# Two multiplies of an FP4 quantization moved from VectorE to GpSimd, with alternating buffers

## The chip, the cores and the metric

One Trainium2 chip, all 8 of its cores. Each core runs the same program on one of 8 batch elements of 2048 tokens with 1024 features; nothing is exchanged between cores. The metric is the device time of the slowest core in microseconds. Engines are named as in the profile: PE is TensorE (matmuls), PEld its weight loads, DVE is VectorE, ACT is ScalarE, POOL is GpSimd, SP is SyncE, which only issues DMAs here.

## What is computed

Two layers, each a product of a mixer and a gated feed-forward, added to its input. The change lies in the feed-forward of the first layer, which quantizes all its operands to FP4 in blocks of 16:

```python
xn = layernorm(x)
s  = attention(xn)                                  # stage 1
def fp4_quant_dequant(x):                           # blocks of 16 along the last dim
    scale = max(max|xb| / 6, 1e-12)
    q = GRID[searchsorted(MID, |xb / scale|)] * sign * scale    # grid 0 .5 1 1.5 2 3 4 6
def fp4_linear(x, w):
    return quant(x) @ quant(w).T
h = silu(fp4_linear(xn, w_gate)) * fp4_linear(xn, w_up)         # stage 2, 2816 hidden columns
x = x + s * silu(fp4_linear(h, w_down))
...                                                 # layer 1: a scan (stage 3) and a mixture
                                                    # of 8 experts (stage 4)
```

## The kernel before

The whole program is written once as a "narrative" (`make_l0_attn`, `make_l0_ffn`, `make_l1_attn`, `make_l1_ffn`), which is run once for each engine and emits only that engine's instructions. So each engine executes its instructions in the order in which they stand in the text, and waits only on semaphores: `ved` counts VectorE's steps, `sed` ScalarE's, `ted` TensorE's, `sx`, `sw` the loads. Between stages every engine waits for every semaphore (`phase_barrier`, L107). Stage 2 is `make_l0_ffn` (L582), and it has four loops.

**x tiles** (L631 to L666), 16 tiles of 128 tokens. SP loads the tile into `xt[i % 2]` (L635). `_emit_layernorm` (L554) takes the statistics on VectorE (L555, L556, L558, L560), the root on ScalarE (L564), the reciprocal and a product on VectorE (L567, L569), and normalizes on ScalarE into `q0` (L574). `_emit_quant` quantizes `q0` into `qbf` (bf16, 128x1024). TensorE makes eight 128x128 transposes into a PSUM bank (L656), and ScalarE evacuates it into `xqT` (L661). Before the layer norm of tile i VectorE waits for the transposes of tile i-1 (L641).

**gate/up slices** (L674 to L800), 5 slices of 512 hidden columns and one of 256. For each, 256 rows of the weights at a time are quantized by `_emit_quant2` (L504, two chains interleaved, all of it on VectorE), transposed (L708) and evacuated (L716, L720). Then come 16 token tiles: eight matmuls for gate (L738) and eight for up (L743), Silu on ScalarE (L752), the product on VectorE into one half of `hh` (L756). After every odd tile (a pair is done) VectorE quantizes the pair, `hh` into `hb`: at once as 1024 columns (L766), or in the last slice as two quantizations of 256 columns (L769, L772). TensorE transposes `hb` (L783), and ScalarE evacuates it into `hqT` (L790, L795). In TensorE's order these transposes stand between the matmuls of this pair and those of the next.

**wd rows** (L807 to L847), 8 rows of 128x2816, each loaded by SP into `wdr` (L815, in the space of `q3`, `q4` and what follows) once the last quantization of the row before has ended, and quantized in pieces of 1024, 1024 and 768 columns (L824), with transposes (L835) and an evacuation (L840). Before each piece VectorE waits for the transposes of the one before (L823), since `hb` is written again.

**down** (L851 to L904): matmuls, Silu, gate and residual. The change doesn't touch it.

`_emit_quant` (L468) is a chain of 13 VectorE operations, each reading what the one before wrote. Its last two, L499 and L501, multiply `t2` by the block scales (an operand repeated 16 times) and then `t1` by `t2` into the bf16 output. Everything up to L496 is called the head below, L499 and L501 the tail.

Of the kernel before, what the change touches and what calls it, by code (L numbers as in the profile page):

```python
# [82 lines left out]
def alloc_sems(nc, names):  # L83
# [4 lines left out]
             "ted", "ved", "sed", "std0", "std1", "stx0", "stx1"]  # L88
# [379 lines left out]
def _emit_quant(p, out_bf, t0, t1, t2, blk, W):  # L468
    nb = W // 16
    bm, hs = blk[:, 0:nb], blk[:, nb:2 * nb]  # L470
# [3 lines left out]
    t2 = t2[:][:, 0:W]  # L474
    p.ve.tensor_reduce(bm.rearrange("p (nb one) -> p nb one", one=1), r3(t0),
# [106 lines left out]
def make_l0_ffn(nc, dram, pq, pfx="b_"):  # L582
# [38 lines left out]
    def narrative(p):  # L621
# [6 lines left out]
        ve_q = []  # L628
        te_tr = []
        ve_evac = []  # L630
        for i in range(NT):  # L631
            sl = i % 2
            if i >= 2:
                p.sy.wait_ge(p.ved.h, ve_q[i - 2])
# [8 lines left out]
            se_xn = p.sed.bump()  # L643
            p.ve.wait_ge(p.sed.h, se_xn)
# [28 lines left out]
        se_htr_evac = None  # L673
        for (hs0, hw) in SLICES:  # L674
            nrc = hw // 128
            for gu in range(2):
                for rp in range(nrc // 2):
# [51 lines left out]
            for tc in range(NT):  # L729
# [33 lines left out]
                if se_htr_evac is not None:  # L763
                    p.ve.wait_ge(p.ted.h, te_htr)
                if hw == 512:
                    _emit_quant(p, hb[:, 0:1024], hh[:][:, 0:1024],  # L766
                                q1, q2, blk, 1024).then_inc(p.ved.h, 1)
                else:
                    _emit_quant(p, hb[:, 0:hw], hh[:][:, 0:hw],  # L769
                                q1, q2, blk, hw)  # L770
                    p.ve.drain()
                    _emit_quant(p, hb[:, 512:512 + hw], hh[:][:, 512:512 + hw],  # L772
                                q3, q4, blk, hw).then_inc(p.ved.h, 1)
                ve_hq = p.ved.bump()
# [3 lines left out]
                p.te.wait_ge(p.ved.h, ve_hq)  # L778
# [9 lines left out]
                te_htr = p.ted.bump()  # L788
                p.se.wait_ge(p.ted.h, te_htr)
# [14 lines left out]
        se_wdtr_evac = {}  # L804
        te_wdtr = None
        pi_k = 0
        for rc in range(ND):  # L807
            if rc == 0:
# [10 lines left out]
            if rc == 0:  # L819
                p.ve.wait_ge(p.ted.h, te_htr)  # L820
# [847 lines left out]
```

## Time and profile before

| | us |
|---|---|
| two runs | 6973.5 and 7301.9, median 7137.7 |
| profiled execution | 6957.9 |
| its span on the slowest core (core 0) | 6956.4 |
| spans of the other seven | 6899.7 to 6953.7 |

The profile is that of core 0. It gives for each engine the busy time, for groups of instructions the mean duration, and for idle time of an engine what ended it. Times within the program are counted from the start of the span. Stage 2 runs from about 1486 to 3820 us. A busy TensorE isn't TensorE at its peak: its clock has two levels, 1.2 and 2.4 GHz, and "PEclk" is the share of the higher one that was granted (0.5 is 1.2 GHz).

### The profile page before, as it was taken

Reading aid. Unit: us, or ns where it says so; the run is one execution under the profiler, and the core shown is the slowest. Engines: PE = TensorE matmul, PEld = TensorE weight load, DVE = VectorE, ACT = ScalarE, POOL = GpSimd, SP = SyncE. Lnnn points to the kernel's source line nnn. Section 1 sums busy time; section 2 is a strip of 40 time slices with the busy share of each in tenths; the row PEclk is TensorE's granted clock in tenths of the full one; section 3 lists DMA queues with packets and bytes.
Section 4 is the critical chain, followed back from the end, with each engine's and each line's share of the span. In section 5 each row is a group of like instructions: output and inputs, shape, how many; then the busy total and the mean of one; then the engine's idle time right before and its main releaser. Section 6 shows DMA issues by size and latency. Waiting matters only on the chain.

```text
span 6956.4 us, 45524 instructions; the slowest of 8 cores (6899.7 to 6956.4 us)
## 1 busy us (share of the span) xinstructions
PE 3609.6 (52%) x15560; PEld 1519.5 (22%) x15560; DVE 2292.4 (33%) x3549; ACT 1256.5 (18%) x2020; POOL 54.1 (1%) x67
## 2 busy tenths in 40 slices
PE   2944445420233233242008055626898898898891
PEld 1410101000111111112004022213343343343340
DVE  2121101047665655646672311223121121121122
ACT  1233333321100001010001321112121121111111
POOL 0000000000000000000000000000000000000000
PEclk9855555555566566576559588857999999999996
DMA  4000000001000000000014412160202202202203
GB/s 88 1 12 0 12 0 12 0 31 36 24 12 12 24 0 24 19 6 7 33 39 146 108 22 24 49 179 16 49 1 49 49 1 49 49 1 49 49 1 142
DMA packets 104753, 248.10 MB, mean 36 GB/s; under 512 B 39984, under 2 KB 40496, under 8 KB 103504
## 3 DMA queue, kind: packets, MB, share of 16 engines
q0 software_dynamic: 62720, 84.73, 8.1%
q1 hardware_dynamic: 41808, 160.45, 6.6%
q8 instruction: 131, 2.15, 0.1%
q14 instruction: 94, 0.77, 0.0%
HBM read 287.80 MB, written 41.94 MB: 47 GB/s over the span
## 4 chain that ended last, share of the span: by engine, by line
PE 49%; DVE 19%; ACT 10%; issue 9%; DMA 9%; DVEq 3%; another core or an unknown queue 0%; SPq 0%; POOL 0%; ACTq 0%; POOLq 0%
PE pq L1416 13%; PE pq L1442 13%; PE pq L1085 4%; PE pq L738 3%; DMA d_b2r<-b_row 3%; PE pq L384 3%; ACT a_expA L357 3%; PE pq L743 2%; ACT a_expB L358 2%; PE pq L342 2%; PE pq L386 2%; PE pq L268 2%; DVE b_q L483 1%; DVE b_q L499 1%; DVE b_q L493 1%
## 5 line engine op out<-in xcount | busy, mean ns | idle before, releaser
L1416 PE MATMUL pq<-d_tT,d_w1e 128*128 128x512 bf16 x4096 | 908.6, 385 | 36.2 <-ACT d_hTh L1424 36.2
L1442 PE MATMUL pq<-d_w2e,d_hTh 128*128 128x512 bf16 x4096 | 889.2, 379 | 33.6 <-ACT d_hTh L1424 33.6
L1458 DVE SCALAR_TENSOR_TENSOR d_acc<-pq,d_comb,d_acc 128x512 f32<-128x512 f32 x256 | 192.2, 751 | 1634.8 <-PE pq L1442 1634.8
L1424 ACT ACTIVATE d_hTh<-pq,d_b1s 128x512 bf16<-128x512 f32 x512 | 352.6, 689 | 1236.5 <-PE pq L1416 1236.5
L1416 PEld LDWEIGHTS pq<-d_tT,d_w1e 128*128 128x128 bf16 x4096 | 404.9, 99 | 538.7 <-issue 68.4
L1442 PEld LDWEIGHTS pq<-d_w2e,d_hTh 128*128 128x128 bf16 x4096 | 398.4, 98 | 524.4 <-issue 48.5
L384 PE MATMUL pq<-a_expA,a_vsb 128*65 128x512 bf16 x320 | 194.3, 607 | 571.6 <-DVE a_expB L369 292.5
L366 DVE TENSOR_TENSOR a_expA<-a_expA,a_masks_s 128x512 bf16<-128x512 bf16 x128 | 54.4, 425 | 965.2 <-ACT a_expB L358 965.2
L783 PE MATMUL pq<-b_ident_s,b_hb 128*128 128x128 bf16 x352 | 45.1, 305 | 611.4 <-DVE b_hb L501 611.4
L1085 PE MATMUL pq<-c_xn2T,c_wsl 128*128 128x512 bf16 x1024 | 263.6, 404 | 162.6 <-ACT c_ga L1095 81.0
L357 ACT ACTIVATE a_expA<-pq 128x512 bf16<-128x512 f32 x320 | 191.2, 597 | 665.3 <-PE pq L346 665.3
L708 PE MATMUL pq<-b_ident_s,b_qbf 128*128 128x128 bf16 x352 | 41.0, 310 | 463.6 <-DVE b_qbf L541 463.6
L738 PE MATMUL pq<-b_wgTs,b_xqT 128*128 128x512 bf16 (+1 forms) x768 | 237.2, 469 | 13.9 <-ACT b_wuTs L720 13.9
L756 DVE TENSOR_TENSOR b_hh<-b_sg,pq 128x512 f32<-128x512 f32 (+1 forms) x96 | 61.7, 643 | 476.9 <-ACT b_sg L752 476.9
L386 PE MATMUL pq<-a_expB,a_vsb 128*65 128x512 bf16 x320 | 202.2, 632 | 0.0
L384 PEld LDWEIGHTS pq<-a_expA,a_vsb 128*65 128x65 bf16 x320 | 42.0, 131 | 724.1 <-issue 724.1
L1461 DVE SCALAR_TENSOR_TENSOR d_acc<-d_b2b,d_comb,d_acc 128x512 f32<-128x512 f32 x256 | 192.3, 751 | 19.7 <-issue 0.9
L342 PE MATMUL pq<-a_qT,a_kT 64*128 64x512 bf16 x320 | 192.9, 603 | 4.1 <-DVE a_s0c L445 3.1
L346 PE MATMUL pq<-a_qT,a_kT 64*128 64x512 bf16 x320 | 193.5, 605 | 0.0
L743 PE MATMUL pq<-b_wuTs,b_xqT 128*128 128x512 bf16 (+1 forms) x768 | 190.4, 397 | 0.0
L358 ACT ACTIVATE a_expB<-pq 128x512 bf16<-128x512 f32 x320 | 189.9, 593 | 0.0
L835 PE MATMUL pq<-b_ident_s,b_hb 128*128 128x128 bf16 x176 | 22.6, 306 | 305.2 <-DVE b_hb L501 305.2
(211 smaller groups left out, 3831.4 us busy)
## 6 DMA issues: line engine op xcount, KB each, us to landing
d_w1e<-w1T POOLq DMA_DIRECT2D x8, 4096.0 KB, 28.3
d_w2e<-w2T POOLq DMA_DIRECT2D x8, 4096.0 KB, 29.0
b_wrow<-wgu SPq DMA_DIRECT2D x44, 512.0 KB, 4.1
b_xt<-x SPq DMA_DIRECT2D x32, 512.0 KB, 4.6
b_wdr<-wd SPq DMA_DIRECT2D x8, 1408.0 KB, 6.4
a_xt<-x SPq DMA_DIRECT2D x16, 512.0 KB, 3.4
s<-a_s0c SPq DMA_DIRECT2D x16, 512.0 KB, 2.6
b_st_<-s SPq DMA_DIRECT2D x16, 512.0 KB, 5.5
```

The lines of the kernel that those rows point to most:

```text
L342: p.te.matmul(sa_[:], kT[0:64, hp * S + kc * 128: hp * S + kc * 128 + 128], qT[0:64, hp * S + qt * 512: hp * S + (qt + 1) * 512], start=Tr ...
L346: p.te.matmul(sb_[:], kT[64:128, hp * S + kc * 128: hp * S + kc * 128 + 128], qT[64:128, hp * S + qt * 512: hp * S + (qt + 1) * 512], star ...
L357: p.se.activation(expA[:, esl * 512:(esl + 1) * 512], sa_[:], AF.Exp)
L358: p.se.activation(expB[:, esl * 512:(esl + 1) * 512], sb_[:], AF.Exp) \
L384: p.te.matmul(pq[4][0:65, :], vA, expA[:, esl * 512:(esl + 1) * 512], start=(kc == 0), stop=(kc == nkc - 1))
L386: p.te.matmul(pq[5][0:65, :], vB, expB[:, esl * 512:(esl + 1) * 512], start=(kc == 0), stop=(kc == nkc - 1)) \
L738: p.te.matmul(gb[:, 0:hw], xqT[:, j * S + tc * 128: j * S + (tc + 1) * 128], wgTs[:, j * 512: j * 512 + hw], start=(j == 0), stop=(j == ND ...
L743: inst = p.te.matmul(ub[:, 0:hw], xqT[:, j * S + tc * 128: j * S + (tc + 1) * 128], wuTs[:, j * 512: j * 512 + hw], start=(j == 0), stop=( ...
L1085: inst = p.te.matmul(bank[:], wsl[sl][:, (w * ND + j) * 128:(w * ND + j + 1) * 128], xn2T[:, j * S + ch * 512: j * S + (ch + 1) * 512], st ...
L1416: inst = p.te.matmul(bank[:], w1e[:, j * MOE_H + hc * 128: j * MOE_H + (hc + 1) * 128], tT[:, j * S + hf * 512: j * S + (hf + 1) * 512], s ...
L1424: p.se.activation(hTh[:, hc * 512:(hc + 1) * 512], bank[:], AF.Gelu, bias=b1s[:, e * 16 + hc: e * 16 + hc + 1]) \
L1442: inst = p.te.matmul(bank[:], hTh[:, j * 512 + tr * 128: j * 512 + (tr + 1) * 128], w2e[:, j * D + dh * 512: j * D + (dh + 1) * 512], star ...
```

## The change

`_emit_quant` keeps its head on VectorE, and its two last multiplies are issued on GpSimd. A new semaphore, `pod`, counts GpSimd's steps: GpSimd waits for the head, multiplies, waits for its own first multiply, multiplies again. `_emit_quant` gets an offset into `blk` (the block scales) and two optional waits: `wait_pod`, which VectorE waits for before the head, and `gp_wait_ted`, which GpSimd waits for before it writes. TensorE now waits for `pod` ahead of the transposes.

In the x tiles `qbf`'s two halves, `blk`'s two parts and the pairs `q1,q2` and `q3,q4` alternate; VectorE doesn't wait for the transposes any more; SP reloads `xt` when ScalarE has normalized it. For the pairs of token tiles the same two sets of buffers alternate (`hb` is still one). `_emit_quant2` stays as it is, but waits for all of GpSimd's work. For `wd` only `q1,q2` are used, so that each head waits for the tail before it; the next `wd` row is loaded once the last head of a row has ended.

```diff
 def _emit_quant(...):
+    if wait_pod:
+        p.ve.wait_ge(p.pod.h, wait_pod)
     ...
     p.ve.tensor_scalar(t2.bitcast(I32), t2.bitcast(I32), 0x7F800000, None,
-                       ALU.bitwise_xor)
-    p.ve.drain()
-    p.ve.tensor_tensor(r3(t2), r3(t2), b3(hs[:]), ALU.mult)
-    p.ve.drain()
-    return p.ve.tensor_tensor(out_bf, t1, t2, ALU.mult)
+                       ALU.bitwise_xor).then_inc(p.ved.h, 1)
+    ved_head = p.ved.bump()
+    p.gp.wait_ge(p.ved.h, ved_head)
+    if gp_wait_ted:
+        p.gp.wait_ge(p.ted.h, gp_wait_ted)
+    p.gp.tensor_tensor(r3(t2), r3(t2), b3(hs[:]), ALU.mult) \
+        .then_inc(p.pod.h, 1)
+    p.gp.wait_ge(p.pod.h, p.pod.bump())
+    p.gp.tensor_tensor(out_bf, t1, t2, ALU.mult).then_inc(p.pod.h, 1)
+    pod_tail = p.pod.bump()
+    return ved_head, pod_tail
...
 # x tiles
             if i >= 2:
-                p.sy.wait_ge(p.ved.h, ve_q[i - 2])
+                p.sy.wait_ge(p.sed.h, se_xn_prev[i - 2])
...
-            if i >= 1:
-                p.ve.wait_ge(p.ted.h, te_tr[i - 1])
...
-            _emit_quant(p, qbf[:, 0:D], q0[:], q1, q2, blk, D).then_inc(p.ved.h, 1)
-            ve_q.append(p.ved.bump())
+            t12 = (q1, q2) if i % 2 == 0 else (q3, q4)
+            vh, pt = _emit_quant(
+                p, qbf[:, (i % 2) * D:(i % 2) * D + D], q0[:], t12[0], t12[1],
+                blk, D, boff=(i % 2) * 256,
+                wait_pod=(quv[i - 2][1] if i >= 2 else None),
+                gp_wait_ted=(te_tr[i - 2] if i >= 2 else None))
...
-            p.te.wait_ge(p.ved.h, ve_q[i])
+            p.te.wait_ge(p.pod.h, pt)
...
 # weights of a slice
-                        blk, [0, 256], D)
+                        blk, [0, 256], D,
+                        wait_pod=(p.pod.v if p.pod.v else None))
...
 # pairs of token tiles
-                if se_htr_evac is not None:
-                    p.ve.wait_ge(p.ted.h, te_htr)
+                par = hq_k % 2
+                t12 = (q1, q2) if par == 0 else (q3, q4)
+                wp = hq_pt.get(hq_k - 2)
+                gwt = hq_te.get(hq_k - 1)
                 if hw == 512:
-                    _emit_quant(p, hb[:, 0:1024], hh[:][:, 0:1024],
-                                q1, q2, blk, 1024).then_inc(p.ved.h, 1)
+                    vh, pt = _emit_quant(p, hb[:, 0:1024], hh[:][:, 0:1024],
+                                         t12[0], t12[1], blk, 1024,
+                                         boff=par * 256, wait_pod=wp,
+                                         gp_wait_ted=gwt)
...
-                p.te.wait_ge(p.ved.h, ve_hq)
+                p.te.wait_ge(p.pod.h, pt)
...
 # wd
-                if te_wdtr is not None:
-                    p.ve.wait_ge(p.ted.h, te_wdtr)
-                _emit_quant(p, hb[:, 0:cw], wdr[:][:, c0:c0 + cw], q1, q2, blk, cw) \
-                    .then_inc(p.ved.h, 1)
-                ve_wdq = p.ved.bump()
+                vh, pt = _emit_quant(
+                    p, hb[:, 0:cw], wdr[:][:, c0:c0 + cw], q1, q2,
+                    blk, cw, boff=0,
+                    wait_pod=wd_pt.get(pi_k - 1),
+                    gp_wait_ted=(te_wdtr if pi_k >= 1 else te_htr))
+                wd_pt[pi_k] = pt
+                ve_wdq = vh
...
-                p.te.wait_ge(p.ved.h, ve_wdq)
+                p.te.wait_ge(p.pod.h, pt)
```

## Rows read from the trace of the kernel before

**Rows 1.** The page, busy us of each engine (share of the span), x instructions

```profile
PE 3609.6 (52%) x15560; PEld 1519.5 (22%) x15560; DVE 2292.4 (33%) x3549; ACT 1256.5 (18%) x2020; POOL 54.1 (1%) x67
```

**Rows 2.** Windows view: stretch, length, busy us of each engine, PEclk, DMA share, GB/s

```profile
1486.00:1757.00 271.00, 15.76 (x126) 12.22 (x127) 197.00 (x304) 39.83 (x48) 0.47 (x1) 0.50 0.10 35
1757.00:3326.00 1569.00, 480.12 (x2244) 244.47 (x2242) 953.71 (x1396) 147.13 (x236) 0.00 (x0) 0.63 0.04 14
3326.00:3656.00 330.00, 23.64 (x181) 17.27 (x180) 231.33 (x312) 23.57 (x26) 0.00 (x0) 0.50 0.10 38
```

**Rows 3.** Waits, 1486 to 3660 us: engine, tile, line, releaser: total us, times, longest

```profile
PE pq L783 <- DVE b_hb L501: 611.4, 48, 13.4
...
PE pq L835 <- DVE b_hb L501: 305.2, 24, 18.5
...
PE pq L656 <- DVE b_qbf L501: 262.8, 16, 29.5
```

**Rows 4.** Timeline, an x tile: start us, us, engine, line, op, operands, count [idle]

```profile
1603.65 0.69 DVE L496 TENSOR_SCALAR b_q<-b_q 128x1024 int32<-128x1024 int32 x1
...
1605.71 1.23 DVE L501 TENSOR_TENSOR b_qbf<-b_q 128x1024 bf16<-128x1024 f32 x1
1607.16 0.77 PEld L656 LDWEIGHTS pq<-b_ident_s,b_qbf 128*128 128x128 bf16 x8 [16.09 <-issue]
1607.19 1.01 PE L656 MATMUL pq<-b_ident_s,b_qbf 128*128 128x128 bf16 x8 [15.86 <-DVE b_qbf L501]
1608.30 1.03 ACT L661 ACTIVATE b_xqT<-pq 128x1024 bf16<-128x1024 bf16 x1 [12.93 <-PE pq L656]
1608.31 0.69 DVE L555 BATCH_NORM_STATS2 b_blk<-b_xt 128x6 f32<-128x512 f32 x1 [1.37 <-PE pq L656]
...
1610.20 0.20 ACT L564 ACTIVATE b_blk<-b_blk 128x1 f32<-128x1 f32 x1 [0.88 <-DVE b_blk L560]
```

**Rows 5.** Timeline, two pairs of 1024 columns

```profile
1876.43 3.29 PE L738 MATMUL pq<-b_wgTs,b_xqT 128*128 128x512 bf16 x8
...
1879.55 1.89 PE L743 MATMUL pq<-b_wuTs,b_xqT 128*128 128x512 bf16 x8
...
1894.35 0.68 DVE L496 TENSOR_SCALAR b_q<-b_q 128x1024 int32<-128x1024 int32 x1
...
1897.86 0.77 PEld L783 LDWEIGHTS pq<-b_ident_s,b_hb 128*128 128x128 bf16 x8 [13.46 <-issue]
...
1898.70 3.62 PE L738 MATMUL pq<-b_wgTs,b_xqT 128*128 128x512 bf16 x8
...
1902.11 2.40 PE L743 MATMUL pq<-b_wuTs,b_xqT 128*128 128x512 bf16 x8
```

**Rows 6.** Timeline, a pair of the 256-column slice

```profile
3264.41 0.42 DVE L475 TENSOR_REDUCE b_blk<-b_hh 128x16 f32<-128x256 f32 x1 [0.16 <-issue]
...
3267.88 0.28 DVE L496 TENSOR_SCALAR b_q<-b_q 128x256 int32<-128x256 int32 x1
...
3274.25 0.34 PEld L783 LDWEIGHTS pq<-b_ident_s,b_hb 128*128 128x128 bf16 x4 [11.28 <-issue]
```

**Rows 7.** Timeline, end of one `wd` row and start of the next

```profile
3446.18 0.55 DVE L496 TENSOR_SCALAR b_q<-b_q 128x768 int32<-128x768 int32 x1
...
3448.90 0.33 SPq L815 DMA_DIRECT2D b_wdr<-wd  x1
...
3455.32 1.22 DVE L475 TENSOR_REDUCE b_blk<-b_wdr 128x64 f32<-128x1024 f32 x1 [6.52 <-DMA b_wdr<-wd]
...
3463.48 0.69 DVE L496 TENSOR_SCALAR b_q<-b_q 128x1024 int32<-128x1024 int32 x1
...
3468.14 1.22 DVE L475 TENSOR_REDUCE b_blk<-b_wdr 128x64 f32<-128x1024 f32 x1 [1.37 <-PE pq L835]
```

**Rows 8.** Groups by line, 1900 to 4700 us: wider and narrower multiplies and additions

```profile
L1113 DVE TENSOR_TENSOR c_gb_<-c_gd,c_gb_ 128x2048 f32<-128x2048 f32 x8 | 18.3, 2293 | 361.6 <-ACT c_gd L1105 361.6
...
L1157 DVE TENSOR_TENSOR c_s1t<-pq,c_obb 128x512 f32<-128x512 f32 x16 | 11.1, 691 | 81.5 <-DMA c_xt<-xn 74.7 <-PE pq L1136 6.8
```

More of the change, by code:

```diff
@@ L465, in make_l0_attn, with _emit_quant @@
     return narrative
-def _emit_quant(p, out_bf, t0, t1, t2, blk, W):
+def _emit_quant(p, out_bf, t0, t1, t2, blk, W, boff=0, wait_pod=None,
+                gp_wait_ted=None):
     nb = W // 16
-    bm, hs = blk[:, 0:nb], blk[:, nb:2 * nb]
+    bm, hs = blk[:, boff:boff + nb], blk[:, boff + nb:boff + 2 * nb]
     r3 = lambda ap: ap.rearrange("p (nb w) -> p nb w", w=16)
@@ L496, in _emit_quant, with _emit_quant2 @@
     p.ve.tensor_scalar(t2.bitcast(I32), t2.bitcast(I32), 0x7F800000, None,
-                       ALU.bitwise_xor)
-    p.ve.drain()
-    p.ve.tensor_tensor(r3(t2), r3(t2), b3(hs[:]), ALU.mult)
-    p.ve.drain()
-    return p.ve.tensor_tensor(out_bf, t1, t2, ALU.mult)
-def _emit_quant2(p, out_bfs, t0s, t1s, t2s, blk, boffs, W):
+                       ALU.bitwise_xor).then_inc(p.ved.h, 1)
[9 more added lines that the diff above has]
+    return ved_head, pod_tail
+def _emit_quant2(p, out_bfs, t0s, t1s, t2s, blk, boffs, W, wait_pod=None):
     nb = W // 16
@@ L507, in _emit_quant2 @@
     b3 = lambda ap: AP(ap.tensor, ap.offset, [list(ap.ap[0]), list(ap.ap[1]), [0, 16]])
+    if wait_pod:
+        p.ve.wait_ge(p.pod.h, wait_pod)
     last = [0, 0]
@@ L628, in narrative @@
         ve_q = []
+        quv = []
+        se_xn_prev = {}
         te_tr = []
@@ L673, in narrative @@
         se_htr_evac = None
+        hq_pt = {}
+        hq_te = {}
+        hq_k = 0
         for (hs0, hw) in SLICES:
@@ L762, in narrative @@
                 p.ve.drain()
-                if se_htr_evac is not None:
-                    p.ve.wait_ge(p.ted.h, te_htr)
+                par = hq_k % 2
+                t12 = (q1, q2) if par == 0 else (q3, q4)
+                wp = hq_pt.get(hq_k - 2)
+                gwt = hq_te.get(hq_k - 1)
                 if hw == 512:
-                    _emit_quant(p, hb[:, 0:1024], hh[:][:, 0:1024],
-                                q1, q2, blk, 1024).then_inc(p.ved.h, 1)
+                    vh, pt = _emit_quant(p, hb[:, 0:1024], hh[:][:, 0:1024],
+                                         t12[0], t12[1], blk, 1024,
+                                         boff=par * 256, wait_pod=wp,
+                                         gp_wait_ted=gwt)
                 else:
+                    wpa = hq_pt.get(hq_k - 1)
                     _emit_quant(p, hb[:, 0:hw], hh[:][:, 0:hw],
[L770 to L774, printed above, removed]
+                                q1, q2, blk, hw, boff=0,
+                                wait_pod=(wpa - 2 if wpa else wp),
+                                gp_wait_ted=gwt)
+                    vh, pt = _emit_quant(p, hb[:, 512:512 + hw],
+                                         hh[:][:, 512:512 + hw],
+                                         q3, q4, blk, hw, boff=256,
+                                         wait_pod=wpa)
+                hq_pt[hq_k] = pt
                 bank = pq[6 + (tc // 2) % 2]
                 pb_bf = bank[:].bitcast(BF16)
-                p.te.wait_ge(p.ved.h, ve_hq)
+                p.te.wait_ge(p.pod.h, pt)
                 if se_htr_evac is not None:
@@ L788, in narrative @@
                 te_htr = p.ted.bump()
+                hq_te[hq_k] = te_htr
+                hq_k += 1
                 p.se.wait_ge(p.ted.h, te_htr)
@@ L804, in narrative @@
         se_wdtr_evac = {}
+        wd_pt = {}
         te_wdtr = None
```

15 lines of the change are left out of this document (11 added, 4 removed).

## The prediction

> **What bounds the kernel now.** I read the page's line of busy times first [rows 1]: no engine is busy for more than 52% of the span and POOL has 67 instructions in all (54.1 us). So there are idle engines, and one has to ask stage by stage who waits for whom. The diff touches only the second stage, which runs from 1486 to 3820 us. The windows view [rows 2] cuts it: the x tiles (1486 to 1757 us, 16 of them), the gate/up slices (1757 to 3326 us) and the quantizing of `wd` (3326 to 3656 us). In all three VectorE is the busiest engine (197 of 271, 954 of 1569, 231 of 330 us), which would suggest that taking two operations off it pays. The view of waits [rows 3] says otherwise: TensorE stood still for 611.4 us over 48 waits at L783 until VectorE had ended L501, 305.2 us over 24 at L835, 262.8 us over 16 at L656. The last multiply of every quantization is what TensorE waits for, and TensorE's queue is in order: the eight transposes of a pair of token tiles stand ahead of the next pair's matmuls. VectorE in its turn has nothing to do until those matmuls come. Quantization, transposes, matmuls, Silu and product form one chain with little overlap. What counts is how late the last multiply ends, not how busy VectorE is.
>
> **The change, part by part.**
>
> *The two multiplies.* L499 and L501 move from VectorE to POOL in 96 calls of `_emit_quant`: 16 x tiles, 40 pairs of 1024 columns, 16 quantizations of 256 columns (8 pairs), 24 pieces of `wd` (16 of 1024, 8 of 768). `_emit_quant2` stays on VectorE. On VectorE they cost, from the end of L496 to TensorE's first weight load, 1897.86 - (1894.35 + 0.68) = 2.83 us [rows 5].
>
> *Price on POOL.* No row of this trace shows POOL computing on a tile (its 54.1 us are DMA issues and memsets of one column). Below, it can't be expected to beat VectorE on the same shape, 1.23 us [rows 4]. The nearest row above is the same operation on VectorE with twice the columns, 2.293 us [rows 8]: that is the cost if the engine takes the two inputs one after the other instead of together. If the output takes a third pass, the step between those two rows (1.07 us for 1024 elements) is added again: 3.36 us, my upper end. I take the middle one, 2.29 us, as an estimate: the lower end supposes that POOL matches VectorE in everything, the upper one that nothing in it goes on side by side. The Trainium skill (GPSIMD Engine Reference, Performance versus the Vector engine) gives 4497 ns for 2048 fp32 columns on GpSimd and so advises VectorE for elementwise work; half of it would be 2.25 us, and the sum below would end 6 us lower. No run here shows it yet.
>
> *Handoffs.* Three per tail: VectorE to POOL, POOL's first multiply to its second (it waits on its own semaphore), POOL to TensorE. The trace has 0.22 us from VectorE to TensorE (1605.71 + 1.23 to 1607.16) and 0.10 us from VectorE to ScalarE or from TensorE to ScalarE (1607.19 + 1.01 to 1608.30) [rows 4]. These are the two ends; I take 0.22 for each, since POOL's multiplies can hardly have less in front of them than TensorE. So a tail of 1024 columns takes 3 x 0.22 + 2 x 2.29 = 5.24 us instead of 2.83: **2.41 us later**.
>
> *Pairs of 1024 columns.* VectorE's next work (L756 of the next pair, or `_emit_quant2` at the end of a slice, which now waits for POOL) needs what comes behind the tail, and TensorE stands at L783. All of it is on the path: 40 x 2.41 = +96.4 us. The two sets `q1,q2` and `q3,q4` buy nothing here, as no head runs under a tail.
>
> *Pairs of 256 columns (last slice).* Here two quantizations follow each other, so the first's tail runs beside the second's head. Before: 3274.25 - 3264.41 = 9.84 us. A head takes 3267.88 + 0.28 - 3264.41 = 3.75 us [rows 6]. After: 2 x 3.75 + 0.08 + 3 x 0.22 + 2 x 0.69 (the 512-column row [rows 8] stands for two inputs of 256) = 9.62 us. Eight times -0.2 us; I put 0. If that cover failed (below) it would be +11 us.
>
> *x tiles.* On paper VectorE is free after the head: it no longer waits 1.37 us for the transposes (L555), nor does two multiplies. But look at ScalarE's order: `Sqrt` (L564) and the normalizing L574 of tile i+1 stand behind the evacuation L661 of tile i, which waits for the transposes, which wait for the tail. Before, from the end of L496 (1604.34) to `Sqrt` at 1610.20: 5.86 us, where the last thing to come was VectorE's statistics [rows 4]. After: the tail 5.24, transposes and evacuation from 1607.16 to 1609.33 = 2.17, together 7.41 us; the statistics (1608.31 to 0.10 us before 1610.20, 1.79 us) are long done under it. +1.55 x 15 = 23.3 us, and the last tile's tail, +2.4. Sum +25.7 us. The stall moves from L555 to L567, where VectorE waits for ScalarE's `Sqrt`. The load of `xt` is released earlier and was hidden before.
>
> *`wd` pieces.* Between pieces `wait_pod` makes the next head wait for POOL's tail, since `q1,q2` are not alternated here: 5.24 us in place of 3468.14 - 3464.17 = 3.97 [rows 7], +1.27 x 16 = +20.3 us. The next row of `wd` is now loaded from the end of the third head, not of its tail: SP's issue comes 3448.90 - 3446.73 = 2.17 us after it today, 0.10 us of which is the handoff. 2.07 us earlier x 7 = -14.5 us, and the third tail (3 x 0.22 + 2 x 1.76, between the rows of 512 and 2048 elements, 4.2 us) hides under the load, for which VectorE waits 6.5 us. The very last tail is seen: +1.9. Sum +7.7 us.
>
> *The rest* (some waits in the barriers, one semaphore) is microseconds at most; the other stages are as they were.
>
> Sum: 96.4 + 0 + 25.7 + 7.7 = **+130 us**. Against the profiled execution's 6957.9 us that is 7088 us, +1.9%. The median before, 7137.7 us, is that of two runs 330 us apart; the profiled one lies by the lower (6973.5), and I forecast for such runs. Faster or slower by 2% (139 us), about what a measurement of this kernel can tell from no change, would be under 6819 or over 7097.
>
> **Rivals.**
>
> *A, slower by over 2%: POOL's multiply is dearer.* It counts 144 times (2 x (40 + 16 + 16)), so 0.07 us more than 2.29 crosses the line: 2.36 us decides. At 2.6 us it is 7088 + 144 x 0.31 = 7133 us, at 3.36 us 7242. For it: nothing in this trace supports 2.29 from above. Against it: handoffs of 0.10 would give back 72 x 3 x 0.12 = 26 us.
>
> *B, POOL multiplies as fast as VectorE (1.23 us).* The tail is 3.12 us: pairs +0.29 x 40 = +12, x tiles -0.57 x 15 + 0.3 = -8, `wd` -0.85 x 16 - 14.5 = -28: 6934 us, within 2%. Even then it isn't faster by 2%: the change can't pay, as it shortens no part of the long chain.
>
> *C, the x tiles overlap after all* (if `Sqrt` were not held): each tile shorter by 1.37 and 2.60 us, 16 times -4.0 = -64 in place of +26: 6999 us. Program order speaks against it.
>
> *D, VectorE and POOL hold each other up.* Tails and heads meet only in the x tiles and the 256-column pairs. If the x tile's statistics had to wait for both multiplies, they would end at 5.02 + 1.89 = 6.9 us, still before 7.41: nothing. In the narrow pairs two short VectorE operations might each wait 0.69 us, 8 x 1.4 = +11 us: 7099 us, part of A. The Trainium skill (SBUF — State Buffer, Who interferes with whom) says that the two engines lock each other out of a shared port for a whole instruction when VectorE runs a 2-port mode or reads two SBUF inputs. By that rule the statistics, with one input, wouldn't even wait; no row here shows it.
>
> *TensorE's clock.* The eight L738 and L743 matmuls after a wait took 3.29 and 1.89 us in one pair, 3.62 and 2.40 us in the next [rows 5]: the clock rises from 1.2 to 2.4 GHz somewhere in the burst, 0.8 us sooner or later. With a new period the mix may shift, at most by some +-30 us over 40 pairs; I see no direction.
>
> **How the numbers follow.** Forecast (multiply between 2.0 and 2.36 us): 0.54. A: 0.40, so high because its line is only 9 us above my sum. B: 0.03, C: 0.02. All mechanisms that bring it under 6819 us together: 0.01. So faster 0.01, within 2% 0.54 + 0.03 + 0.02 = 0.59, slower 0.40. Low end: handoffs at 0.10 (-26) and the clock at its best (-27): 7035 us. High end: a multiply halfway to the upper end, 2.83 us (+78), and some 19 us of clock and lockouts: 7185 us. The forecast's own range is 7035 to 7097.
>
> **What would show it.** POOL 128x1024 multiplies near 2.3 us, 144 of them, and start to start near 2.5; from the end of L496 to the transposes about 5.2 us; TensorE's wait at L783 up by about 2.4 us a pair; in the x tiles 1.55 us more a tile than today's 16.9 (271 / 16, the first load in it), with ScalarE's `Sqrt` right behind the evacuation; `wd` rows of about 41 us (330 / 8) as before. x tiles of 13 us would prove my reading of ScalarE's queue wrong, and an unchanged wait at L783 the one of the chain.

## The result, and the profile after

The changed kernel takes 1.010 times as long as the one before (95% interval 1.006 to 1.014): the median over 11 runs is 7041.1 us, against 6960.2 over 10. The ratio is smaller than that of the medians because it leaves out the runs in which the cores of one die were disturbed. The profiled execution took 6996.7 us. I had forecast 7088 us, +130 us or +1.9%, inside the 2% that count as no change, for executions like the profiled one. The sign and the class are right. The time is not: the median lies just above the low end of my range (7035 us), but the profiled execution, which is what I forecast, lies 38 us below it (four more runs took 6996.5 to 7000.9 us), and the loss in stage 2 is 79 us where I had worked out 130.

The whole program, and where the loss is, as the median over the eight cores. The times are differences of start times in the records: x tiles from the first `L555` (L566 after) to the first weight reduction, slices from there to the first reduction over `wd`, wd from there to the first matmul of the down loop, the rest after that.

| us | start of stage 2 | x tiles | slices | wd | rest |
|---|---|---|---|---|---|
| before | 1457 | 266.4 | 1576.4 | 319.7 | 3293 |
| after | 1457 | 285.8 | 1637.5 | 318.0 | 3293 |
| change | 0 | +19.5 | +61.1 | -1.7 | 0 |
| forecast | | +25.7 | +96.4 | +7.7 | 0 |

Stage 2 is 79 us longer. The spans on the two pages differ by 39 us only, because in the profiled execution before, the slowest core (0) started stage 2 at 1491 us, core 1 at 1489 and the other six at about 1457: the first stage of core 0, which the change doesn't touch, was 34 us late.

The page of the changed kernel, the line of busy times:

```profile
PE 3550.1 (51%) x15560; PEld 1505.2 (22%) x15560; DVE 2089.9 (30%) x3357; ACT 1251.9 (18%) x2020; POOL 409.5 (6%) x259
```

Beside [rows 1], VectorE was relieved of 202 us of its 2292, and POOL took over 355. No engine was the bound, and none is now. The view of waits (1486 to 3760 us, same columns as [rows 3]) shows where the relief went:

```profile
PE pq L816 <- POOL b_hb L508: 690.6, 48, 15.4
DVE b_hh L781 <- ACT b_sg L777: 631.4, 96, 12.7
...
PE pq L874 <- POOL b_hb L508: 301.6, 24, 19.8
...
PE pq L674 <- POOL b_qbf L508: 250.8, 15, 17.2
...
DVE b_blk L578 <- ACT b_blk L575: 78.6, 14, 6.2
...
DVE b_blk L478 <- POOL b_hb L508: 75.8, 16, 5.0
...
DVE b_blk L527 <- POOL b_hb L508: 23.6, 5, 4.7
```

TensorE's wait ahead of the transposes of a pair (L816, formerly L783) grew from 611.4 to 690.6 us [rows 3], and its releaser is now POOL; in the x tiles (L674, formerly L656) it grew by 1.2 us a tile, from 15.6 (233.3 over 15, without the first) to 16.7 (250.8 over 15), and in the `wd` rows (L874, formerly L835) it stayed (305.2 and 301.6). VectorE's wait for Silu, ahead of its product (L781), was this before:

```profile
DVE b_hh L756 <- ACT b_sg L752: 476.9, 96, 13.0
```

It grew by 154 us, more than any other wait of VectorE: in the pairs VectorE waits for what comes behind the tail. The three last rows are new waits of VectorE: for ScalarE's `Sqrt` in the x tiles (78.6 us over 14), for POOL between the pieces of `wd` (75.8 over 16) and for POOL at the start of a slice (23.6 over 5). VectorE's saved time has become its waiting time.

The two multiplies, by form (engine, operands, count, busy us, mean ns):

```profile
L505 POOL TENSOR_TENSOR b_q<-b_q,b_blk 128x1024 f32<-128x1024 f32 x72 | 139.1, 1932 | 1659.2 <-DVE b_q L499 1659.2
L508 POOL TENSOR_TENSOR b_hb<-b_q 128x1024 bf16<-128x1024 f32 x56 | 131.0, 2340 | 8.3 <-POOL b_q L505 0.4
```

1.93 us with the operand that is repeated 16 times, 2.34 us for the plain one into bf16. The Trainium skill (GPSIMD Engine Reference, Performance versus the Vector engine) gives 1.96 times VectorE's time for a two-input addition of 2048 fp32 columns. The plain multiply here, 2.34 against 1.22 us, is 1.9 times and agrees; the other, 1.93 us, is 1.6 times and better than that.

The timeline of an x tile after (start, us, engine, line):

```profile
1579.07 2.34 POOL L508 TENSOR_TENSOR b_qbf<-b_q 128x1024 bf16<-128x1024 f32 x1
1581.63 0.77 PEld L674 LDWEIGHTS pq<-b_ident_s,b_qbf 128*128 128x128 bf16 x8 [17.17 <-issue]
...
1582.77 1.02 ACT L681 ACTIVATE b_xqT<-pq 128x1024 bf16<-128x1024 bf16 x1 [14.99 <-PE pq L674]
1583.69 0.19 ACT L575 ACTIVATE b_blk<-b_blk 128x1 f32<-128x1 f32 x1
...
1594.06 0.69 DVE L499 TENSOR_SCALAR b_q<-b_q 128x1024 int32<-128x1024 int32 x1
1594.66 0.69 DVE L566 BATCH_NORM_STATS2 b_blk<-b_xt 128x6 f32<-128x512 f32 x1
1594.95 1.93 POOL L505 TENSOR_TENSOR b_q<-b_q,b_blk 128x1024 f32<-128x1024 f32 x1 [13.53 <-DVE b_q L499]
...
1596.29 0.15 DVE L571 TENSOR_SCALAR b_blk<-b_blk 128x1 f32<-128x1 f32 x1
1597.02 2.34 POOL L508 TENSOR_TENSOR b_qbf<-b_q 128x1024 bf16<-128x1024 f32 x1
```

Here the chain of the prediction is to be read line by line: the tail (L505, L508) ends at 1581.41, the transposes follow 0.22 us later, ScalarE evacuates (L681) and only then takes the root (L575) for which VectorE's statistics had long been ready; in the next tile the statistics end at 1596.44 (L571) while POOL has just got to the middle of its tail.

### The profile page after: what moved, and what is told of

The parts are those of the page before. It is cut to its first block, busy times and chain, and to the rows that moved or that the text cites. A ratio compares the mean times of both kernels' runs of the same rounds, so it can differ in the third digit from the quotient of the medians.

```text
span 6995.2 us, 45641 instructions; the slowest of 8 cores (6980.3 to 6995.2 us)
## 1 busy us (share of the span) xinstructions
PE 3550.1 (51%) x15560; PEld 1505.2 (22%) x15560; DVE 2089.9 (30%) x3357; ACT 1251.9 (18%) x2020; POOL 409.5 (6%) x259
## 4 chain that ended last, share of the span: by engine, by line
PE 48%; DVE 17%; ACT 10%; issue 9%; DMA 8%; POOL 5%; DVEq 2%; another core or an unknown queue 0%; SPq 0%; ACTq 0%; POOLq 0%
PE pq L1455 13%; PE pq L1481 13%; PE pq L1124 4%; PE pq L763 3%; PE pq L384 3%; DMA d_b2r<-b_row 3%; ACT a_expA L357 3%; PE pq L768 2%; ACT a_expB L358 2%; PE pq L342 2%; POOL b_q L505 2%; POOL b_hb L508 2%; PE pq L386 2%; PE pq L268 2%; DVE b_q L486 1%
## 5 line engine op out<-in xcount | busy, mean ns | idle before, releaser
L816 PE MATMUL pq<-b_ident_s,b_hb 128*128 128x128 bf16 x352 | 45.1, 305 | 690.6 <-POOL b_hb L508 690.6
L505 POOL TENSOR_TENSOR b_q<-b_q,b_blk 128x1024 f32<-128x1024 f32 (+2 forms) x96 | 161.0, 1677 | 1875.6 <-DVE b_q L499 1875.6
L781 DVE TENSOR_TENSOR b_hh<-b_sg,pq 128x512 f32<-128x512 f32 (+1 forms) x96 | 61.7, 643 | 631.4 <-ACT b_sg L777 631.4
L763 PE MATMUL pq<-b_wgTs,b_xqT 128*128 128x512 bf16 (+1 forms) x768 | 228.9, 456 | 13.7 <-ACT b_wuTs L745 13.7
L816 PEld LDWEIGHTS pq<-b_ident_s,b_hb 128*128 128x128 bf16 x352 | 33.7, 136 | 711.2 <-issue 711.2
```

The source lines that it names most:

```text
L505: p.gp.tensor_tensor(r3(t2), r3(t2), b3(hs[:]), ALU.mult) \
L763: p.te.matmul(gb[:, 0:hw], xqT[:, j * S + tc * 128: j * S + (tc + 1) * 128], wgTs[:, j * 512: j * 512 + hw], start=(j == 0), stop=(j == ND ...
```

## The experiments

All stage times below are made as in the table above. The "period" is the time from one head to the next. "Tail" is the time from the end of the head to TensorE's first weight load behind it, "burst" from there to the next head, both in the wide pairs, as means over the records (before: 2.83 and 11.39 us; after: 4.84 and 10.88).

**One part alone: the x tiles.** The tail is emitted by a switch; everything else multiplies on VectorE with the changed kernel's buffers. (In every kernel whose `wd` tails are on VectorE, the load of the next `wd` row waits for the last multiply again, not for the end of the head.)

```diff
+    if tail == "ve":
+        if gp_wait_ted:
+            p.ve.wait_ge(p.ted.h, gp_wait_ted)
+        p.ve.drain()
+        p.ve.tensor_tensor(r3(t2), r3(t2), b3(hs[:]), ALU.mult)
+        p.ve.drain()
+        p.ve.tensor_tensor(out_bf, t1, t2, ALU.mult).then_inc(p.pod.h, 1)
+        return ved_head, p.pod.bump()
```

> Only the x tiles keep their tail on GpSimd; pairs and wd multiply on VectorE again. Theory (the chain through ScalarE's queue): the x tiles take 285.8 us as in the changed kernel (266.3 before), the slices 1577 us and wd 320 us as before, so that the kernel ends about 20 us later than the one before. Rival (the x tiles' loss is caused by something in the later loops or in the code's size): x tiles near 266 us.

Measured: x tiles 285.8 us on every core, to the tenth that of the changed kernel. On cores 4 to 7, whose mean granted clock was 0.726 to 0.727 (0.710 to 0.714 on the others), the slices took 1576.8 us, as before, and wd 299.4. The loss of the x tiles comes from the x tiles. My guess of wd "as before" was wrong by 20 us: the wait for the transposes no longer stood ahead of the head there either.

**One part alone: the pairs.** Same switch, `tail="ve"` in the x tiles and for wd.

> Only the pairs of token tiles keep their tail on GpSimd. Theory (each tail is on the chain, 2.0 us longer, and TensorE's burst 0.5 us shorter): slices 1637 us as in the changed kernel against 1577 before, mean burst 10.9 us. x tiles: the tail is back on VectorE but qbf has two halves, so VectorE doesn't wait for the transposes; ScalarE's order then decides: 2.83 + 2.17 + 0.01 = 5.0 us from head to Sqrt in place of 5.86, 0.85 x 15 = 13 us less, 253 us. Rival (no queue at ScalarE: VectorE is free at once): 1.37 us less a tile, 246 us. wd: VectorE doesn't wait for transposes before a head but ahead of its last multiplies, where they are long done: 16 x 1.37 = 22 us less than before, 298 us.

Measured: slices 1635.0 us (after 1637.5), tail 4.84, burst 10.82; x tiles 252.9 and wd 298.7 us, both as expected. So the changed buffers and waits alone, with the multiplies left on VectorE, gain 13.5 us in the x tiles and 21 us in wd. Moving the multiplies costs 33 and 19 us in the same loops; the 19 us are what is left of 32 us between the pieces, as the earlier load of the next `wd` row, which comes with the move, gives 14 back.

**Lateness without GpSimd.** No multiply on GpSimd; in the wide pairs VectorE's tail is padded to GpSimd's length.

```diff
+        if pad:
+            p.ve.tensor_tensor(out_bf, t1, t2, ALU.mult)
+            p.ve.drain()
+            p.ve.tensor_scalar(t1, t1, 1.0, None, ALU.mult)
+            p.ve.drain()
         p.ve.tensor_tensor(out_bf, t1, t2, ALU.mult).then_inc(p.pod.h, 1)
```

> No multiply on GpSimd at all; in the pairs of 1024 columns VectorE repeats its last multiply and a multiply by 1 (+2.07 us in the tail, same result), so that the tail is 4.9 us, as long as on GpSimd. Theory (only the lateness counts, and the burst gets shorter because the period of the pairs changes TensorE's clock pattern): slices near 1637 us, mean burst 10.9 us instead of 11.4. Rival (the burst is shorter because VectorE's port or queue is freer with GpSimd doing the work): burst stays at 11.4 us, slices 1577 + 40 x 2.07 = 1660 us. x tiles 253, wd 298 us as in the pairs-only kernel.

Measured: tail 4.91, burst 10.65, slices 1633.6 us. The padded VectorE kernel costs the slices as much as the changed one, and the shorter burst is there too, without any work on GpSimd. The rival (1660 us) is out. Group rows of the matmuls of gate and up, in the kernel before (L738, L743), the changed one (L763, L768) and the padded one (L777, L782): line, operands, count, busy us, mean ns, idle before.

```profile
L738 PE MATMUL pq<-b_wgTs,b_xqT 128*128 128x512 bf16 (+1 forms) x768 | 237.2, 469 | 13.9 <-ACT b_wuTs L720 13.9
...
L743 PE MATMUL pq<-b_wuTs,b_xqT 128*128 128x512 bf16 (+1 forms) x768 | 190.4, 397 | 0.0
```

```profile
L763 PE MATMUL pq<-b_wgTs,b_xqT 128*128 128x512 bf16 (+1 forms) x768 | 228.9, 456 | 13.7 <-ACT b_wuTs L745 13.7
...
L768 PE MATMUL pq<-b_wuTs,b_xqT 128*128 128x512 bf16 (+1 forms) x768 | 179.4, 380 | 0.0
```

```profile
L777 PE MATMUL pq<-b_wgTs,b_xqT 128*128 128x512 bf16 (+1 forms) x768 | 224.8, 451 | 13.7 <-ACT b_wuTs L759 13.7
...
L782 PE MATMUL pq<-b_wuTs,b_xqT 128*128 128x512 bf16 (+1 forms) x768 | 176.9, 377 | 0.0
```

The matmuls are the same 768 each; the mean of gate's falls from 469 ns to 456 and 451, that of up's from 397 to 380 and 377. Both groups together are 19 us shorter in the changed kernel.

**Twice the padding.**

> As the padded kernel, with the padding twice: VectorE's tail in the pairs is 7.0 us, 2.07 more. If TensorE's burst gets shorter with a longer tail in general, it stays at 10.7 us or falls and the period is 26.1 us. If the burst depends on how the period falls on the clock's pattern, it can come out anywhere between 10.5 and 12.4 us, the ends seen among the pairs of the kernel before.

Measured: tail 6.98, burst 11.79 us, period 27.3, slices 1756 us. Its matmuls:

```profile
L782 PE MATMUL pq<-b_wgTs,b_xqT 128*128 128x512 bf16 (+1 forms) x748 | 239.8, 480 | 17.3 <-ACT b_wuTs L764 15.6 <-issue 1.1
...
L787 PE MATMUL pq<-b_wuTs,b_xqT 128*128 128x512 bf16 (+1 forms) x753 | 196.8, 408 | 1.8 <-issue 1.4
```

480 and 408 ns: with 2.07 us more of waiting ahead of it, TensorE's burst got 1.1 us longer, not shorter. So a longer wait doesn't shorten the burst in general.

What changes is the clock. At the first weight load of every wide burst the granted clock is 0.5 (1.2 GHz), and it rises to 1.0 (2.4 GHz) somewhere between 2.6 and 6.1 us later. Two bursts of the kernel before, in the windows view (columns as in [rows 2]), from the first weight load to the next head:

```profile
1989.39:2001.45 12.06, 10.39 (x40) 4.52 (x40) 1.38 (x2) 2.28 (x4) 0.00 (x0) 0.76 0.00 0
2012.78:2023.40 10.62, 8.95 (x40) 4.17 (x40) 1.37 (x2) 2.28 (x4) 0.00 (x0) 0.86 0.00 0
```

In the first the rise came 5.9 us after the weight load, in the second 3.0 us. Read in this way from the clock records of every burst (the mean of each core's, then the median over the cores), the rise came at 4.51 us before the change, at 3.50 after it, at 3.04 with the padding and at 5.35 with twice the padding (there cores 0 to 5). Over the 35 bursts of a core of the first two kernels, each us of later rise makes the burst about 0.5 us longer, and a straight line misses their lengths by under 0.1 us (root mean square). So the 1.0 us by which the rise came earlier is the 0.5 us by which the burst got shorter.

Why the rise comes where it does is not shown. In the kernel before the bursts run 10.5 to 12.4 us in a pattern that nearly repeats (10.95, 11.75, 11.98, 10.59, 11.56, 12.06, 10.62); in the changed kernel they mostly drift from 11.2 down to 10.6, with a jump to 12.1 in some slices. That fits a rise whose place depends on how the period of the pairs falls on something periodic in the clock's control; what that is, and which periods are lucky, these four points (22.7, 24.1, 24.2 and 27.3 us) don't settle.

**The price by itself.** A stretch ahead of the x tiles, with tiles of ones: four of each form on POOL, VectorE idle; then the plain form beside VectorE.

```python
p.gp.tensor_tensor(q3[:], q1[:], q2[:], ALU.mult)                  # L653
p.gp.tensor_tensor(r3(q3[:]), r3(q1[:]), b3, ALU.mult)             # L657
p.gp.tensor_tensor(qbf[:, 0:D], q1[:], q2[:], ALU.mult)            # L661
p.gp.tensor_tensor(r3(qbf[:, 0:D]), r3(q1[:]), b3, ALU.mult)       # L665
p.gp.tensor_scalar(q3[:], q1[:], 1.0, None, ALU.mult)              # L669
# the form of L653 again, beside VectorE's
#   L676: tensor_reduce (L679)  L688: tensor_scalar (L691)  L698: tensor_tensor (L701)
```

> The changed kernel with a stretch ahead of the x tiles in which GpSimd multiplies tiles of ones: two f32 inputs to f32, one of them repeated 16 times, each also to bf16, and one input times a constant, VectorE idle; then the first form again beside VectorE's reductions (one input), one-input multiplies in f32 and two-input multiplies. In the changed kernel the multiply with a repeated input takes 1.93 us and the one to bf16 2.34 us. If the repeated input is what is cheap: 2.3 / 1.93 / 2.34 / 1.93 us. If the bf16 output is what is dear: 1.93 / 1.93 / 2.34 / 2.34 us. Beside VectorE: by theory free beside the reductions (under 5% longer); beside one-input multiplies and two-input multiplies each waits for the other, so GpSimd's start-to-start grows by about one VectorE instruction (0.7 or 1.2 us) or VectorE's by one of GpSimd's. Rival: no effect in any of the three. It adds about 100 us to the kernel, which is not of interest.

Groups on POOL (busy us, mean ns):

```profile
L698 POOL TENSOR_TENSOR b_q<-b_q 128x1024 f32<-128x1024 f32 x4 | 12.8, 3200 | 8.4 <-DVE b_st_ L691 8.0
...
L669 POOL TENSOR_SCALAR b_q<-b_q 128x1024 f32<-128x1024 f32 x4 | 11.1, 2767 | 0.7 <-POOL b_q L669 0.5 <-POOL b_qbf L665 0.2
L688 POOL TENSOR_TENSOR b_q<-b_q 128x1024 f32<-128x1024 f32 x4 | 10.7, 2668 | 1.2 <-DVE b_blk L679 0.8
...
L676 POOL TENSOR_TENSOR b_q<-b_q 128x1024 f32<-128x1024 f32 x4 | 9.4, 2346 | 0.6 <-POOL b_q L669 0.2
L661 POOL TENSOR_TENSOR b_qbf<-b_q 128x1024 bf16<-128x1024 f32 x4 | 9.4, 2338 | 0.6
L653 POOL TENSOR_TENSOR b_q<-b_q 128x1024 f32<-128x1024 f32 x4 | 9.3, 2337 | 8.9 <-DVE b_blk L649 8.5
...
L657 POOL TENSOR_TENSOR b_q<-b_q,b_blk 128x1024 f32<-128x1024 f32 x4 | 7.7, 1930 | 0.6
L665 POOL TENSOR_TENSOR b_qbf<-b_q,b_blk 128x1024 bf16<-128x1024 f32 x4 | 7.7, 1930 | 0.6
```

The repeated input is what is cheap (1.93 with either output); the bf16 output costs nothing (2.34 with either). One input times a constant takes longer than two inputs, 2.77 us. And VectorE's side, the line's view (durations in ns, min/median/max), for the reductions, the one-input and the two-input multiplies:

```profile
L679 DVE TENSOR_REDUCE b_blk<-b_gt x8: 1219/1220/1220, 1508.9 to 1518.1; 128x64 f32<-128x1024 f32 x8
```

```profile
L691 DVE TENSOR_SCALAR b_st_<-b_gt x14: 693/695/2642, 1519.5 to 1537.7; 128x1024 f32<-128x1024 f32 x14
```

```profile
L701 DVE TENSOR_TENSOR b_x1t<-b_gt,b_hh x8: 1224/2200/3176, 1538.6 to 1555.7; 128x1024 f32<-128x1024 f32 x8
```

Beside the reductions nothing changes on either side (2.35 and 1.22 us). Beside one-input multiplies POOL's go from 2.34 to 2.67 us and VectorE's from 0.69 to 2.64 us while both run; beside two-input ones to 3.20 and 3.18. They take turns, whole instructions at a time. The Trainium skill (SBUF — State Buffer, Who interferes with whom) has it that whoever issues first gets the shared ports for the whole instruction, that a one-input multiply in a 2-port mode and a multiply with both inputs in SBUF can be held in this way, and that a reduction never is. By these rows it holds.

**The queue at ScalarE.** The changed kernel, with the evacuation of x tile i-1 emitted behind the norm of tile i.

```diff
             se_xn_prev[i] = se_xn
+            if i >= 1:
+                evac_x(i - 1)      # wait for te_tr[i - 1], then the activation into xqT
 ...
-            p.se.wait_ge(p.ted.h, te_tr[i])
-            p.se.activation(strided_ap(xqT, i * 128, ...), ...)
```

> The changed kernel, but in the x tiles ScalarE evacuates tile i-1 after it has normalized tile i, not before. Theory (ScalarE's queue is what hides the free VectorE): VectorE goes from the end of the head (8.53 us) straight to the next statistics, 4.03 us until the next head: a period of 12.7 us instead of 17.7, x tiles about 16 x 12.7 + 6 = 209 us instead of 285.8; the kernel 77 us faster than the changed one, about on a par with or slightly faster than the one before. Rival (GpSimd's multiplies hold up the statistics or the next head on VectorE): period 14 us or more, x tiles 230 us or more. Slices and wd as in the changed kernel, 1637 and 318 us.

Measured: x tiles 239.7 us, 46 less than in the changed kernel, not 77; slices 1636.7. The whole is at 1.006 times the time before (1.002 to 1.010); the changed kernel's 1.010 has an interval that overlaps. ScalarE's queue was the cover, as the prediction said, but behind it lay another:

```profile
1571.29 0.69 DVE L574 BATCH_NORM_STATS2 b_blk<-b_xt 128x6 f32<-128x512 f32 x1
...
1572.64 0.21 DVE L577 BATCH_NORM_AGGREGATE b_blk<-b_blk 128x2 f32<-128x12 f32 x1
...
1573.17 0.20 ACT L583 ACTIVATE b_blk<-b_blk 128x1 f32<-128x1 f32 x1 [9.44 <-DVE b_blk L579]
...
1573.65 2.34 POOL L516 TENSOR_TENSOR b_qbf<-b_q 128x1024 bf16<-128x1024 f32 x1
1573.72 2.29 DVE L588 SCALAR_TENSOR_TENSOR b_blk<-b_blk 128x1 f32<-128x1 f32 x1
```

`Sqrt` (L583) now comes right after the statistics. But L588, a product of one column that takes 0.16 us before and after, takes 2.29 us: it starts 0.07 us behind POOL's second multiply and ends with it. The rival that I had called harmless (D) costs 2.1 us a tile once the queue doesn't hide it: from the end of a head to the next head it is 6.15 us, where I expected 4.03.

**The order at TensorE.** All multiplies on VectorE; the transposes and the evacuation of pair k are emitted behind the matmuls of pair k+1.

```diff
                 te_gu = p.ted.bump()
+                if tc % 2 == 1 and pend is not None:
+                    trans_h()      # wait for the tail of the pair before, its 8 transposes
 ...
                 se_sg = p.sed.bump()
+                if tc % 2 == 1 and pend is not None:
+                    evac_h()       # its evacuation into hqT, behind this pair's Silu
```

> All multiplies on VectorE (two buffer sets as in the changed kernel), and in the pairs TensorE's transposes and ScalarE's evacuation of pair k stand behind the matmuls of pair k+1. Theory (the order in TensorE's queue is the bound, not any engine): VectorE is busy all through, 8.53 + 2.6 + two products 1.6 us = 12.8 us a pair instead of 22.7; 35 x 9.9 = 350 us less in the wide slices, some 40 in the narrow one, slices about 1190 us, kernel about 6530 us. Rival (the chain over two pairs, tail, transposes, matmuls, head, 22.7 us for two, is what binds): the same or 11.4 us, so VectorE decides. A rival that would show me wrong: VectorE isn't free to start early and the slices stay over 1500 us.

Measured: slices 1171.5 us instead of 1576, period 12.49 us; the kernel is at 0.936 (0.921 to 0.952). A pair in the timeline:

```profile
1879.68 1.28 DVE L834 TENSOR_TENSOR b_hh<-b_sg,pq 128x512 f32<-128x512 f32 x2
...
1880.02 0.61 PE L775 MATMUL pq<-b_ident_s,b_hb 128*128 128x128 bf16 x8 [3.64 <-DVE b_hb L508]
...
1880.51 3.57 PE L812 MATMUL pq<-b_wgTs,b_xqT 128*128 128x512 bf16 x8
...
1881.12 1.22 DVE L478 TENSOR_REDUCE b_blk<-b_hh 128x64 f32<-128x1024 f32 x1 [0.16 <-issue]
...
1891.02 1.23 DVE L508 TENSOR_TENSOR b_hb<-b_q 128x1024 bf16<-128x1024 f32 x1
1892.16 1.28 DVE L834 TENSOR_TENSOR b_hh<-b_sg,pq 128x512 f32<-128x512 f32 x2
...
1892.50 0.61 PE L775 MATMUL pq<-b_ident_s,b_hb 128*128 128x128 bf16 x8 [3.24 <-DVE b_hb L508]
```

VectorE goes from its last multiply (L508) to both products (L834) to the next head (L478) with at most 0.16 us between them; the matmuls (L812) run under the head.

**The same order with the tails on GpSimd.**

> The changed kernel (tails on GpSimd) with the same order in TensorE's queue as in the late-transposes kernel. Theory: now VectorE needs only 10.2 us a pair, but tail, transposes, matmuls and head make 24.2 us for two pairs, 12.1 each, and where GpSimd's multiplies lie beside VectorE's they lock each other out (a one-input VectorE multiply takes 2.64 in place of 0.69 us), up to 2 us a pair: 12.1 to 14 us, slices 1170 to 1240 us, so no gain over VectorE's own multiplies. Rival (once the order is right the move pays, because VectorE is the bound): 10.2 us a pair, slices about 1100 us, 80 us less than with VectorE's multiplies.

Measured: slices 1159.0 us, period 11.9; kernel 0.942 (0.934 to 0.949), since the x tiles (285.8) and wd (318.8) have the tails on GpSimd as well. In the wide pairs the move now pays 0.6 us a pair of the some 2.5 that it takes off VectorE. Where the rest goes:

```profile
1884.75 1.22 DVE L478 TENSOR_REDUCE b_blk<-b_hh 128x64 f32<-128x1024 f32 x1 [0.16 <-issue]
1885.46 2.34 POOL L516 TENSOR_TENSOR b_hb<-b_q 128x1024 bf16<-128x1024 f32 x1
1886.04 1.80 DVE L481 TENSOR_SCALAR b_blk<-b_blk 128x64 f32<-128x64 f32 x1
...
1888.03 0.77 PEld L775 LDWEIGHTS pq<-b_ident_s,b_hb 128*128 128x128 bf16 x8 [5.42 <-issue]
```

L481 works on 64 columns and takes 0.20 us; here it takes 1.80, to the end of POOL's L516, and over the 35 wide periods of this core 0.94 on average, 0.75 more than without GpSimd's work. For another 1.0 us a pair VectorE stands still (2.0 us in place of 0.95 in the kernel with its own multiplies), mostly ahead of a product that waits for Silu: that is the chain over two pairs, 24 us for two.

**All loops freed, VectorE alone and with GpSimd.** On top of the late transposes: the norm of x tile i+1 ahead of the quantization of tile i (`hh` as second `q0`), the reload of a weight row pair at its last reading (step 4 of `_emit_quant2`), and two buffers for `wd` rows.

```diff
+        norm_x(0)
         for i in range(NT):
+            if i + 1 < NT:
+                norm_x(i + 1)
 ...
-                    ve_wq[wk - 2] = vq
+                    ve_wq[wk - 2] = vread
 ...
-            if rc >= 1:
-                p.sy.wait_ge(p.pod.h, wd_pt[pi_k - 1])
+            wdb = [wdr, wdr2][rc % 2]
+            if rc >= 2:
+                p.sy.wait_ge(p.pod.h, wd_pt[pi_k - 4])
```

> All multiplies on VectorE, transposes one pair late as in e4, and the other loops freed of their waits too: the norm of x tile i+1 is issued ahead of the quantization of tile i (second buffer for q0), a weight row pair is reloaded once it has been read for the last time instead of at the end of its quantization, wd rows have two buffers. Theory (order and waits were the bound, VectorE is what is left): x tiles 11.2 + 2.6 = 13.8 us each, 225 us in place of 253; 16 waits of 5.3 us for weights fall away, slices 1171 - 80 = 1090 us; wd rows 31 + waits of under 1 us, 255 us in place of 299. Sum 150 us less than e4's 6533 us: about 6380 us, ratio to the kernel before 0.92. Rival (another wait takes the place of those removed, as in the changed kernel): under 80 us less.

Measured: x tiles 230.2 us (225 expected), wd 255.9 us, as expected; slices 1126.2, a gain of 45 us and not 80. The wait for the load had covered another, for the transposes of the rows before, which now shows as 36.7 us in the waits:

```profile
DVE b_blk L535 <- PE pq L754: 36.7, 16, 2.3
```

The profiled execution took 6444.7 us, 7.4% under the profiled one before, and the shortest run 6376.6 us; there is no ratio with an interval for this kernel.

> The same, with the tails of the x tiles and the pairs on GpSimd (wd on VectorE). It is the arrangement in which the move should pay if it ever does, since VectorE is what is left as the bound. Without any lockout VectorE saves 2.6 us in 16 x tiles and up to 2.6 us in 40 pairs, 42 + 104 = 146 us; the pairs already came out at 11.9 us against 12.5 with VectorE's multiplies, 0.6 x 35 = 21 us. Theory (GpSimd and VectorE lock each other out wherever VectorE has a one-input f32 multiply or two inputs from SBUF): the gain is small, 10 to 40 us against e8. Rival (lockouts are short): 80 us or more against e8.

Measured: slices 1107.0 us, 19 less than with VectorE's multiplies, but x tiles 260.1 us, 30 more; kernel 0.921 (0.909 to 0.932).

```profile
DVE b_blk L588 <- ACT b_blk L585: 79.4, 16, 5.8
```

The row is my own slip: here the evacuation stands ahead of the next-but-one `Sqrt`, and with GpSimd's longer tail the wait for it opens. VectorE waits 79.4 us over 16 tiles (L588), against 14.9 us with its own multiplies. It is the same trap as in the change itself. So in the arrangement made for it the move gains 19 us in the slices and loses 30 in the x tiles, 11 us longer in all where I had expected 10 to 40 us less. The shortest runs say the same, 6392.4 us against 6376.6. With the evacuation moved as well it might have kept the 19 us; that was not run.

## Why the prediction was right or wrong

**What bounds the kernel: right.** TensorE's wait ahead of the transposes grew by what the tail grew; making the tail as late on VectorE costs the same, and taking the transposes out of the way gives 405 us with the same work.

**The base: 34 us too high.** I added my sum to 6957.9 us, the profiled execution, in which core 0 came late into stage 2; the lowest runs before take 6924 us. Of the 91 us between my 7088 and the measured 6996.7, 34 are this base, 51 the sum, and the rest lies in stages that the change doesn't touch. But even from a base 34 us lower the measured time would lie just under the low end, so the sum has to answer too. Two of its terms are the steps that failed.

**The term of the tail: mis-sized.** I put 5.24 us for a wide tail, and it is 4.84. Of the 0.40 us, 0.31 is the price of the multiplies, 2 x 2.29 put and 1.93 + 2.34 measured. I priced both by one row though they differ in their operand; the row of twice the columns was right for the plain one within 0.05 us, and the repeated input is cheaper. The other 0.09 us are the handoffs: 0.20, 0.14 and 0.22 us against three of 0.22. So the pairs lose 2.01 us each and not 2.41, 16 us in all, and with the x tiles (6 us) and `wd` (9 us) this term makes up some 31 of the 51 us.

**The term of TensorE's clock: put at nothing.** I wrote that the mix may shift by up to 30 us and that I saw no direction, and left it at zero. It came to -0.51 us a pair, 40 x 0.51 = 20 us, the rest of the 51. Together with the tail, 40 x (2.01 - 0.51) = 60 us, which is the measured +61. That the shift isn't GpSimd's doing, nor what a longer tail brings in general, is what the two padded kernels show (10.65 us at one period, 11.79 at another); in that sense it was luck. The bound was right; that it can be as large as a sixth of the forecast should have been said in the sum.

**Narrow pairs: right.** Forecast -0.2 us each, measured 9.91 to 9.85 us from the first reduction to the weight load. The lockout (the two engines holding each other up) shows in L481, 0.45 us at most where it takes 0.17 otherwise, and in L486, 0.64 against 0.42: about 0.5 us a pair, already in the 9.85.

**x tiles: the mechanism right.** From the end of a head to the next head the mean went from 8.04 to 9.22 us, +1.18, against +1.55 forecast; less the 0.40 of the tail it is the forecast. That there is no effect of the lockout (D) was right for this kernel only because ScalarE's queue is later still, and D looked at the wrong operation: the statistics don't wait for POOL (0.69 us beside it), the product of one column does.

**wd: right but for the tail.** From the end of a head to the next 4.74 us against 5.24 put, 3.97 before: +0.77 x 16 = 12 us; the load issued earlier took 2.16 us off each change of rows (8.47 to 6.31), where 2.07 was forecast, 15 us. Sum, with the last tail, about -1; measured -1.7.

**Rivals.** A (a dearer multiply) is out: 1.93 and 2.34 us. So is B (as fast as VectorE's 1.23). C did not happen, for the reason given; the kernel with ScalarE's order changed for it took 239.7 us for the x tiles, where C comes to 266.4 - 64 = 202, as it ran into D. I gave A 0.40 because my sum stood 9 us from its line. With the measured 1.93 and 2.34 and my own handoffs the same sum gives 108 us, 31 below the line, so A's weight came from a price that no row could give.

## What to carry to other kernels

Before moving work off a busy engine, ask what is queued behind it on the engines that consume it: here TensorE's transposes stood ahead of the next matmuls and ScalarE's evacuation ahead of the next root, so that a freed VectorE could only wait. Moving the transposes and their evacuation in the text gave, with the new buffers, 6.4%, where moving 202 us of multiplies lost 1%. GpSimd's two-input work, at 1.6 to 1.9 times VectorE's time, paid only in the slices and only once the transposes were out of the way (12.5 and 19 us), and even there VectorE's short instructions had to take turns with it. And where TensorE starts each burst of a loop at 1.2 GHz, the place of the rise is a term of its own (0.5 to 1.1 us a pair between these kernels): put its spread into the sum, not only into the range. Take the base from a core, or a run, that isn't late for another reason.

## What the runs showed of the hardware

- On POOL a multiply of 128x1024 f32 takes 2.34 us, 1.93 if one input is repeated 16 times, with an f32 and with a bf16 output alike; times a constant it takes 2.77 us, more than with two inputs. Start to start, each waiting on the one before, is 0.14 us more.
- POOL and VectorE take turns by whole instructions when VectorE multiplies in f32, with one input or two (0.69 to 2.64 us, 1.22 to 3.18), and even a product of one column waits (0.16 to 2.29 us), as does a one-input operation on 64 columns (0.20 to 1.80). A reduction isn't touched (1.22), nor are the statistics of the layer norm (0.69 us beside POOL's multiply).
- In the wide bursts the granted clock rose from 0.5 to 1.0 between 2.6 and 6.1 us after the first weight load, and each us later made the burst about 0.5 us longer: 10.65 to 11.79 us on average for the same 32 matmuls and 8 transposes in four kernels with different tails.
